# Sorted projection: leaf numbers packed six to a register and loaded once, in place of a register load for every four tiles

## The reference, cut to what matters

```python
def _fff(x, node_w, node_b, w1, b1, w2, b2):
    cur = jnp.zeros((N,), jnp.int32)
    for _ in range(DEPTH):
        pw = node_w[cur]
        score = jnp.einsum('nd,nd->n', xf, pw) + node_b[cur]
        cur = 2 * cur + 1 + (score >= 0).astype(jnp.int32)
    leaf = cur - N_NODES
    sel = jax.nn.one_hot(leaf, N_LEAVES, dtype=xf.dtype)
    hidden_all = jax.nn.relu(jnp.einsum('nd,ldh->lnh', xf, w1) + b1[:, None, :])
    hidden = hidden_all * sel.T[:, :, None]
    out = jnp.einsum('lnh,lho->no', hidden, w2) + sel @ b2
    return out.reshape(Bx, Sx, D)
...
q, k, v = (_fff(x, ...) for each of the three sets of weights)
attn = jax.nn.softmax(jnp.einsum('bqd,bkd->bqk', q, k) * scale, axis=-1)
return jnp.einsum('bqk,bkd->bqd', attn, v)
```

## Time and profile before

| | |
|---|---|
| median of three runs | 3102.98 us |
| runs | 3110.54, 3101.52, 3102.98 us |
| the profiled execution's own time | 3097.87 us |
| its span in the profile | 3096.1 us |
| mean granted TensorE clock | 0.956 |
| PE busy | 2846.5 us, 92% of the span |
| DVE busy | 2127.4 us, 69% |
| ACT busy | 1796.9 us, 58% |
| POOL busy | 909.8 us, 29% |

### The profile page before, as it was taken

One profiled execution on the slowest core, in us unless ns is written; L12 is line 12 of the kernel. 1 busy time (PEld: TensorE's weight loads), 2 busy tenths in 40 slices (PEclk: granted clock), 3 DMA queues, 4 the chain that ended last, 5 costly groups with the idle time before them and its releaser, 6 DMA issues. The chain is left out here.

```text
span 3096.1 us, 55570 instructions
## 1 busy us (share of the span) xinstructions
PE 2846.5 (92%) x20746; PEld 1731.8 (56%) x20746; DVE 2127.4 (69%) x3331; ACT 1796.9 (58%) x3503; POOL 909.8 (29%) x1482
## 2 busy tenths in 40 slices
PE   5788999998799999999999999999795588899999
PEld 2676888886643333333333333333253377688888
DVE  5445555445689999999999999998054444555544
ACT  3445343334338888888888888888543344443333
POOL 4552310001353333333333333311112554230000
PEclk8999999998869999999999999999897799999999
DMA  8795211105945544445555554442234589220010
GB/s 248 240 289 162 67 41 32 31 25 174 298 52 67 67 61 54 59 59 63 67 67 67 67 63 56 49 48 32 80 101 131 170 283 279 77 64 30 30 31 21
DMA packets 447349, 302.08 MB, mean 98 GB/s; under 512 B 170712, under 2 KB 421692, under 8 KB 447084
## 3 DMA queue, kind: packets, MB, share of 16 engines
q1 hardware_dynamic: 413164, 214.59, 35.0%
q0 software_dynamic: 33920, 83.93, 8.5%
HBM read 183.27 MB, written 118.78 MB: 98 GB/s over the span
## 5 line engine op out<-in xcount | busy, mean ns | idle before, releaser
L1531 DVE TENSOR_REDUCE mx_ha<-s_ps_ha 128x2 f32<-128x1024 f32 x1024 | 1244.0, 1223 | 61.3 <-PE s_ps_ha L1438 55.1
L1596 ACT ACTIVATE probs_ha<-s_ps_ha 128x512 f32<-128x512 f32 x2048 | 1108.8, 595 | 192.7 <-PE s_ps_ha L1449 58.8
L1438 PE MATMUL s_ps_ha<-ks_ha,qs_ha 48*128 48x512 f32 x2048 | 760.3, 455 | 16.6 <-POOL onesr_ha L1404 11.8
L1449 PE MATMUL s_ps_ha<-qs_ha,ks_ha 50*128 50x512 f32 x2048 | 749.8, 446 | 0.9 <-ACT probs_ha L1596 0.2
L1460 PE MATMUL o_ps_ha<-probs_ha,vs_ha 128*32 128x256 f32 (+1 forms) x7936 | 646.7, 398 | 0.9 <-DVE oT_ha L1558 0.9
L1438 PEld LDWEIGHTS s_ps_ha<-ks_ha,qs_ha 48*128 48x128 f32 x2048 | 313.3, 190 | 444.2 <-DVE mx_ha L1531 372.5
L863 ACT ACTIVATE probsT_a<-pT_ps_a 128x512 fp32r<-128x512 f32 x256 | 146.4, 597 | 423.2 <-PE pT_ps_a L737 408.2
L1460 PEld LDWEIGHTS o_ps_ha<-probs_ha,vs_ha 128*32 128x32 f32 x7936 | 156.5, 108 | 359.9 <-issue 185.8
L1449 PEld LDWEIGHTS s_ps_ha<-qs_ha,ks_ha 50*128 50x128 f32 x2048 | 304.9, 185 | 33.0 <-ACT probs_ha L1596 32.5
L692 POOL DMA_INDIRECT rows_a<-ys_d,slots x96 | 91.0, 948 | 630.8 <-PE turn_ps_a L714 577.7
L1388 POOL TENSOR_TENSOR onorm_ha<-oT_ha,rinv_ha 128x256 f32<-128x256 f32 x32 | 19.9, 622 | 837.1 <-DVE rinv_ha L1561 837.1
(11 more groups left out here) (210 smaller groups left out, 3946.0 us busy)
## 6 DMA issues: line engine op xcount, KB each, us to landing
xs_p<-xs_d SPq DMA_DIRECT2D x282, 128.0 KB
ys_d<-y_p SPq DMA_DIRECT2D x66, 512.0 KB
qs_ha<-parts_d SPq DMA_DIRECT2D x192, 128.0 KB, 6.2
ks_ha<-parts_d SPq DMA_DIRECT2D x192, 128.0 KB, 7.2
parts_d<-parts_hp POOLq DMA_DIRECT2D x32, 512.0 KB, 6.5
xs_d<-y_p SPq DMA_DIRECT2D x6, 1024.0 KB
leaf_w_p<-in_wa SPq DMA_DIRECT2D x4, 1048.0 KB
leaf_w_p<-in_wb SPq DMA_DIRECT2D x4, 1040.0 KB
```

Source lines behind the costliest of these rows:

```text
L1438: nc.tensor.matmul(s1_ps[:, e % BANKS, :], qs[0:QKROWS, n % SLOTS, c, :], ks[0:QKROWS, n % SLOTS, g * 4:(g + 1) * 4, :].rearrange("p c t - ...
L1449: nc.tensor.matmul(out, ks[LOW:LOW + KR, n % SLOTS, c, :], qs[LOW:LOW + KR, n % SLOTS, g * 4:(g + 1) * 4, :].rearrange("p c t -> p (c t)") ...
L1531: nc.vector.reduce_max(mx[:, at:at + 2], s1_ps[:, e % BANKS:e % BANKS + 2, :], AX_X).then_inc(s1_free, 1)
L1596: nc.scalar.activation(probs[:, (n + c) % (LATE + 1), g * 512:(g + 1) * 512], s2_ps[:, turn % TURNS, :], ACT.Exp).then_inc(s2_free, 1)
```

## The change

The leaf numbers are no longer stored as one offset for each tile but packed, six numbers of four bits to a 32-bit integer: eight integers for a head, 24 in all. The packing is done by the matmul that turned the column into a row: its moving operand is now `pack`, a 48 x 8 constant with powers of 16, one more load among the constants (nine in place of eight). DVE's multiplication by LW falls away, PE has three matmuls of 48 columns and three of 8 in place of six of 48, and the one cast becomes two: `row_at` (144 numbers, on which SP waits as before) and `leaves_at` (24 numbers; PE and DVE wait for both). PE and DVE each load all 24 integers into 24 registers in one load ahead of the tiles, and none of the loads in the loop is left. For each tile both now shift, mask and multiply in their sequencer. SP keeps its loads of four registers for each group.

```diff
+NIBBLES = 6
+PACKS = SEGS // NIBBLES
...
-        tile_at = sb("tile_at", [1, 2, FF, SEGS], I32)
+        row_at = sb("row_at", [1, FF, SEGS], I32)
+        leaves_at = sb("leaves_at", [1, FF * PACKS], I32)
+        pack = sb("pack", [SEGS, PACKS])
...
-                 (base[:, :, :], w["base"]), (base2[:, :], w["base2"])]
+                 (base[:, :, :], w["base"]), (base2[:, :], w["base2"]), (pack[:, :], w["pack"])]
...
-                sp.reg_load(at, tile_at[0:1, 0, f, j:j + GROUP])
+                sp.reg_load(at, row_at[0:1, f, j:j + GROUP])
...
-                nc.vector.tensor_scalar(found[:, 1, :], found[:, 1, :], float(LW), None, ALU.mult).then_inc(list_step, 1)
+                dve.wait_ge(list_step, 5)
+                nc.vector.tensor_reduce(found[:, 0, :], owned[:, :, :], AX_X, ALU.add).then_inc(list_step, 1)
                 dve.wait_ge(list_step, 6)
-                nc.vector.tensor_reduce(found[:, 0, :], owned[:, :, :], AX_X, ALU.add).then_inc(list_step, 1)
-                dve.wait_ge(list_step, 7)
                 nc.vector.tensor_tensor(found[:, 0, :], found[:, 0, :], mark[:, :], ALU.add).then_inc(list_step, 1)
                 dve.wait_ge(listed, 1)
-                nc.vector.tensor_copy(tile_at[:, :, :, :].rearrange("p a f s -> p (a f s)"),
-                                      route_ps[0:1, 0:2 * FF * SEGS]).then_inc(tiles_set, 1)
+                nc.vector.tensor_copy(row_at[:, :, :].rearrange("p f s -> p (f s)"),
+                                      route_ps[0:1, 0:FF * SEGS]).then_inc(tiles_set, 1)
+                nc.vector.tensor_copy(leaves_at[:, :], route_ps[0:1, FF * SEGS:FF * (SEGS + PACKS)]).then_inc(tiles_set, 1)
...
                 if n == 0:
-                    dve.wait_ge(tiles_set, 1)
-                if j % GROUP == 0:
-                    dve.reg_load(leaves, tile_at[0:1, 1, f, j:j + GROUP])
-                at = dve.snap(leaves[j % GROUP], min_val=0, max_val=(LEAVES - 1) * LW)
+                    dve.wait_ge(tiles_set, 2)
+                    dve.reg_load(leaves, leaves_at[0:1, :])
+                packed = dve.snap(leaves[f * PACKS + j // NIBBLES])
+                at = dve.snap((packed >> j % NIBBLES * 4 & LEAVES - 1) * LW, min_val=0, max_val=(LEAVES - 1) * LW)
...
             def list_tiles():
-                pe.wait_ge(list_step, 8)
-                for k in range(2 * FF):
-                    last = nc.tensor.matmul(route_ps[0:1, k * SEGS:(k + 1) * SEGS], found[:, k // FF, k % FF:k % FF + 1],
-                                            ident[0:SEGS, 0:SEGS], start=True, stop=True)
+                pe.wait_ge(list_step, 7)
+                for f in range(FF):
+                    nc.tensor.matmul(route_ps[0:1, f * SEGS:(f + 1) * SEGS], found[:, 0, f:f + 1],
+                                     ident[0:SEGS, 0:SEGS], start=True, stop=True)
+                for f in range(FF):
+                    at = FF * SEGS + f * PACKS
+                    last = nc.tensor.matmul(route_ps[0:1, at:at + PACKS], found[:, 1, f:f + 1], pack[:, :], start=True, stop=True)
                 last.then_inc(listed, 1)
-                pe.wait_ge(tiles_set, 1)
+                pe.wait_ge(tiles_set, 2)
...
             def leaf_offset(n, leaves):
-                f, j, g = place(n)
-                if j % GROUP == 0:
-                    pe.reg_load(leaves[g % 2], tile_at[0:1, 1, f, j:j + GROUP])
-                return pe.snap(leaves[g % 2][j % GROUP], min_val=0, max_val=(LEAVES - 1) * LW)
+                f, j, _ = place(n)
+                packed = pe.snap(leaves[f * PACKS + j // NIBBLES])
+                return pe.snap((packed >> j % NIBBLES * 4 & LEAVES - 1) * LW, min_val=0, max_val=(LEAVES - 1) * LW)
...
-                leaves = [[held.enter_context(pe.register(f"leaf{u}{k}_{tag}")) for k in range(GROUP)] for u in range(2)]
+                leaves = [held.enter_context(pe.register(f"leaf{k}_{tag}")) for k in range(FF * PACKS)]
+                pe.reg_load(leaves, leaves_at[0:1, :])
                 turn(0)
                 turn(1)
```

More of the change, by code:

```diff
@@ L424, in _ @@
             with ExitStack() as held:
-                leaves = [held.enter_context(dve.register(f"own{k}_{tag}")) for k in range(GROUP)]
+                leaves = [held.enter_context(dve.register(f"own{k}_{tag}")) for k in range(FF * PACKS)]
                 for n in range(2):
@@ L1978, in arrays_of @@
     w["tri"] = np.triu(np.ones((P, P)), 1).astype(bf16)
+    pack = np.zeros((SEGS, PACKS), np.float32)
+    for j in range(SEGS):
+        pack[j, j // NIBBLES] = LEAVES ** (j % NIBBLES)
+    w["pack"] = pack
     w["marks"] = P * np.arange(SEGS, dtype=np.float32)[:, None]
```

## The result

| | before | after |
|---|---|---|
| median of 12 runs | 3106.26 us | 3099.43 us |
| ratio after to before | | 0.9972, 95% interval 0.9959 to 0.9984 |
| profiled execution, span | 3097.87, 3096.1 us | 3088.07, 3086.3 us |
| first to last first-layer matmul, loop 1 and 2 | 191.1, 191.7 us | 184.4, 186.2 us |

The change makes the kernel 8.7 us faster by the ratio (5.0 to 12.7 by the interval; the medians are 6.8 us apart), under the 9.3 us that a single measurement can tell from nothing. The forecast was 22.8 us. The loops in them lost 12.2 us, so that is where the gain is; they are measured here to the last pass of the last tile, 0.3 us more than in the earlier trace rows.

The account below looks back on a forecast made before the run. PE was taken to set the pace, with the DMA engines a second limit mid-loop. Terms -20.0 - 4.0 + 1.0 - 0.3 + 0.5 = -22.8 us took 3103.0 to about 3080 us, range 3066 to 3099.

Parts of the forecast that it names:

- The bound and the boundary's mechanism: Tile loops: PE sets the pace; at each four-tile boundary DVE's register load delays the weights' copy PE needs, 0.44 us.
- The sign for being wrong that the prediction named: End of first loop: calm groups keeping 4.7 us without loads would show DVE's load was not PE's wait.
- The price of 0.40 us: Lost time per four-tile group at the first loop's calm end, with one PE and one DVE load: 0.40 us.
- the second rival: All 70 boundaries of both loops cost 0.60 us each, 42 us saved, giving 3062 us; chance 0.09.
- The 50 boundaries outside them are taken at the calm price: Both loops outside the DMA-saturated stretches: 50 boundaries each give back 0.40 us, -20.0 us.
- 20 boundaries in saturated stretches x 0.20: Middle of both loops, DMA engines 95% busy: half the price comes back at 20 boundaries, -4.0 us.
- The first rival: DMA and stores take over: saturated boundaries give nothing, the others half, giving 3094 us; chance 0.16.
- Unpacking, +1.0: DVE's shift, mask and product per tile delay only slow weights' copies: +1.0 us, between 0 and +8.
- My third rival's rule: DVE unpacking: n added register instructions delay the weights' copy about 0.1 n - 0.14 us; n = 7 gives 3155 us; chance 0.07.
- The long load: Ahead of the tiles: loading 24 registers takes 2.0 to 7.5 us, hidden under 4.8 us of cover, costing 0.
- The small terms: Outside the tile loops: less list work on DVE and PE, -0.3 us; one more constant load on SP, +0.5 us.

Follow-up runs that it names:

- e1: Kernel before with only PE's leaf numbers packed and loaded once, DVE still loading four registers per group: 3114.01 us, ratio 1.0011.
- e2: Kernel before with only DVE's leaf numbers packed and loaded once, PE still loading four registers per group: 3105.96 us, ratio 0.9984.
- e9: Changed kernel without scatters, third forest using the first's weights, POOL's gathers held until the last turn: 3124.15 us, ratio 1.0123.
- e10: Kernel before without scatters, third forest using the first's weights, POOL's gathers held until the last turn: 3152.61 us, ratio 1.0212.
- e5: Changed kernel with POOL's scatters left out, later forests taking the first's rows: 3069.04 us, ratio 0.9869.
- e6: Kernel before with POOL's scatters left out, later forests taking the first's rows: 3087.68 us, ratio 0.9937.
- r13: Kernel before run again, unaltered, in a later session: 3087.66 us, ratio 0.9993.
- r14: Changed kernel run again, unaltered, in a later session: 3069.47 us, ratio 0.9934.
- r15: Changed kernel with DVE's place_tokens blocks moved ahead of the tile loop: 3059.53 us, ratio 0.9908.
- r16: Kernel before with DVE's place_tokens blocks moved ahead of the tile loop: 3081.84 us, ratio 0.9981.
- e7: Changed kernel with three y buffers for two and nothing else: 3102.77 us, ratio 0.9981.
- r17: Changed kernel with place_tokens ahead of the loop and three y buffers: 3056.78 us, ratio 0.9910.
- The calm pair: e9 and e10, the changed kernel and the kernel before with only row loads and y stores left on the DMA queues: 3124.15 and 3152.61 us.
- e12: Changed kernel with nine pairs of shifts added to DVE's unpacking for each tile: 3131.73 us, ratio 1.0148.
- r18: Changed kernel with three pairs of shifts added to DVE's unpacking for each tile: 3077.45 us, ratio 0.9972.
- e3: Changed kernel with three y buffers and the third forest's weights issued by POOL instead of SP: 3110.08 us, ratio 1.0003.
- e4: Kernel before with three y buffers and the third forest's weights issued by POOL instead of SP: 3116.82 us, ratio 1.0015.

## Why the prediction was wrong

**The bound and the boundary's mechanism: right.** DVE's load between y copy and weights' copy was what PE waited for. Without it the calm steps are 1.09 us at every tile, four in 4.36 (4.4 forecast), and the last 20 steps of e1 and e2 (3.6 and 0.4 us late) show that it was DVE's. The sign for being wrong that the prediction named, calm groups that keep their 4.7 us, did not come.

**The price of 0.40 us: right.** It was read from seven calm groups; e9 and e10 give 0.38 over 70 boundaries and e5 and e6 0.45 over 20. Against the second rival I held that most of the other lateness sits at places without a load; by the split 38.9 of 75.1 us stood at boundary steps, half of it, and 32.7 came back there. The rival's 42 us did not come, since the other steps took 20.5.

**"The 50 boundaries outside them are taken at the calm price": the step that failed.** It took a price, read where nothing else is late, as a gain of the whole loop also where other things are. Of -20.0 the first two profiles gave 13.4: 6.8 of 8.0 us in the last 40 steps, but 6.6 of 12.0 in the first 60. There the boundary steps gave back 18.4 us and the other steps grew by 11.8. What took it can be told for steps 21 to 40 alone. With the scatters gone (e5, e6) their two blocks paid 4.5 and 4.6, where the kernels themselves gave 2.2 and 3.0. With the scatters there but without pauses (r13, r14) the first of them paid 4.9. So in steps 21 to 40 half of the gain was lost with the pauses, and not by the scatters as such; in steps 41 to 60 without pauses it stays open (1.3 in r13 and r14, 4.8 in r15 and r16, one profile each). In the first 20, e5 and e6, which have no pauses there either, paid 4.0, and the first two profiles 1.4. That the stretch at 85 to 133 us has a DMA share of 0.80 was my reason to call it unsaturated; PE was farther from full there (38.94 of 48) than in the saturated one (45.40 of 51), and that was the row to heed.

**"20 boundaries in saturated stretches x 0.20": also failed, by the smaller amount.** -4.0 forecast, +1.2 measured in steps 61 to 100 of the first two profiles, +2.0 in r13 and r14, so this does not hang on the pauses. The boundary steps gave 4.6 us of it in the first two and the others took 5.8. The first rival named the place: DVE's wait for stores in the first loop went from 5.2 to 12.5 us, 11.4 of it between 150 and 215 us, DMA share still 0.95. But the third buffer took that wait away and gave nothing (e7, r17), so the store's wait is not the cause. The rival's figure of 3094 us was nearer in the gain than the forecast (8.8 us for 8.7), which is luck: it had the other boundaries at half for no reason that it gave. The calm pair got 7.3 us in these steps, so the traffic took it; whether the third forest's weights or POOL's gathers, no run separates.

**Where the forecast would have been right.** In the session of r13 and r14 the change is worth 20.4 us (14.5 to 26.2), and 22.8 lies inside. That would have been luck in part, since steps 61 to 100 gave nothing there either.

**Unpacking, +1.0: right in size; the slack was larger than I had it.** In the last 20 steps nothing is left (-0.1), slow copies included (a step of 1.12 us). My third rival's rule put n = 7 at 0.56 us of delay and 76 us. e12's 0.75 us of delay, about 130 us by the same rule, cost 57 in the loops, so the rule was more than twice too dear. r18's 0.26 us cost 8 in the median and 1.8 in the last 20 steps of both loops, where the changed kernel has none: 0.045 us a step, so most of another 0.26 us still fits, and 0.75 does not.

**The long load: 1.81 to 2.07 us, hidden.** On PE (1.81 to 1.83) it lay under the low bound of 2.0 to 7.5. It is 0.08 us a register, and under the cover of 4.8 us. By the Trainium skill's figure (Runtime: NRT & Kernel Launch, instruction fetch mechanics) 24 registers would be 4.8 us, an estimate. The trace does not agree; the page speaks of registers loaded from HBM, and this load reads SBUF.

**The small terms.** The list's cast and the constant's load are too small to be found: program outside the loops moved by +2.4 us in the profiled executions (9.8 less 12.2) and such a difference is within the scatter of two runs. Summed: 24.0 forecast from the loops, 12.2 measured; -22.8 in all, -8.7 measured with an interval from 5.0 to 12.7. The median of 3099.43 us stands just above the upper end of the range, 3099.

**What is not settled.** Why several engines pause for about a microsecond while POOL issues scatters or gathers, in every profile of the earlier sessions and in none of the later, is not known. The runs show that the pauses up to tile 81 go with the scatters, and that neither a y buffer (e7, 65 pauses) nor SP's issue of the weights (e3, 80) ends them. What the earlier and the later sessions differ in was not found. Whether e3 and e4 lost by POOL's own two DMAs a piece was not tried apart.

## What to carry to other kernels

A price per event that is read in a calm stretch holds for calm stretches only. Before multiplying it, sort the events by what else is late within a step or two of each, and where the pacing engine is far from full (here 81% and 89% busy) don't book the gain before something shows that the other lateness is not waiting behind it: the first 60 steps gave 6.6 of 12.0 us, and 8.7 in the later session, and steps 61 to 100 less than nothing of 8.0 in both. Compare only what was measured side by side: the same change was worth 8.7 us in one session and 20.4 in another. Look for what remains beside the change: moving one long block off DVE's path (place_tokens, ratio 0.9908 in all) gave 9.9 us on top, more than the change itself gave at first, and the two together are as fast as anything here that computes the whole result; a third y buffer adds nothing that can be measured.

## What the runs showed of the hardware

- The same two kernels compare as 0.9972 in one session and 0.9934 in another, intervals apart, and the kernel before took 3106 to 3110 us in the earlier sessions and 3085 to 3087 in the later. Chip number 6 stands at both.
- Pauses of several engines together, about 1 us each, in the earlier sessions alone: ACT took up the first layer's result more than 0.3 us late at 22 to 80 tiles of each of ten profiles, and at none in ten later ones. They stood only where POOL issues indirect DMAs.
- One load of 24 registers took 1.81 us on PE and 1.85 to 2.07 on DVE; a load of four 0.33 us at least and 0.70 in the median while the engine was in the loop.
- Merged register instructions take time by what they hold: 57 ns in the changed kernel, 0.21 us in the median of e12, where more shifts were merged into each.
- Two engines' loads at one boundary cost as one where nothing else is late: in the last 20 steps taking PE's away alone gave nothing (3.6 us late for 3.4), DVE's alone 3.0 of 3.5 us. Over both loops DVE's alone gave 8.5 of 12.2 us.
